# Routing and experts of a soft mixture: fused affine layer norm on VectorE, weight split on GpSimd, second product two steps behind

## The reference, cut to what matters

```python
xn = _layernorm(x, ln_gamma, ln_beta)      # (x - m) * rsqrt(var + eps) * gamma + beta
x_unit = _l2norm(xn, axis=-1)
mu_unit = _l2norm(mu, axis=0)
logits = einsum('bnd,des->bnes', x_unit * scale, mu_unit)
dispatch = softmax(logits, axis=1)                         # over the tokens
combine = softmax(logits.reshape(B, N, E * S), axis=-1)    # over the slots
slot_in = einsum('bnd,bnes->besd', xn, dispatch)
h = gelu(einsum('besd,edh->besh', slot_in, w1) + b1)       # per expert
slot_out = einsum('besh,ehd->besd', h, w2) + b2
out = einsum('besd,bnes->bnd', slot_out, combine)          # x + out is returned
```

## Time and profile before

| | |
|---|---|
| median of 3 runs | 1244.21 us (1241.42 to 1247.08) |
| profiled execution | 1238.86 us, of which the span in the trace is 1236.7 us |
| busy over the span | PE 86%, DVE 74%, ACT 58%, POOL 35% |
| route, about 987 to 1140 us of the span | 16 batches |
| experts, about 1141 to 1194 us | 16 experts |
| combine, about 1194 us to the end | 16 batches |

### The profile page before, as it was taken

The page is one execution under the profiler, slowest core; times in us unless marked ns, Lnnn a source line. Parts: engine busy times, 40 slices in busy tenths (PEclk is TensorE's granted clock), DMA queues, the critical chain, the costliest instruction groups (busy, mean ns, idle before and its releaser), DMA issues. The chain is left out here.

```text
span 1236.7 us, 28303 instructions
## 1 busy us (share of the span) xinstructions
PE 1064.9 (86%) x8053; PEld 1014.9 (82%) x8053; DVE 920.8 (74%) x2388; ACT 715.7 (58%) x2225; POOL 438.3 (35%) x753
## 2 busy tenths in 40 slices
PE   7779999999999997899999548888888747777998
PEld 6679999999999996899999547787887647676777
DVE  4567677777677765777777649989899769997656
ACT  4466666676666664333333237777777526566754
POOL 0223222223222220121212136666566466663015
PEclk9889999999999999899999859888888969889559
DMA  7578940000000000000000235444455000000113
GB/s 236 129 133 243 114 101 0 0 0 0 0 0 0 0 1 6 27 0 0 0 0 0 63 111 153 143 133 140 140 140 146 17 15 2 0 0 1 43 32 122
DMA packets 71574, 73.90 MB, mean 60 GB/s; under 512 B 23025, under 2 KB 63829, under 8 KB 71381
## 3 DMA queue, kind: packets, MB, share of 16 engines
q1 hardware_dynamic: 70692, 72.47, 23.4%
q10 hardware_dynamic: 816, 0.66, 0.2%
HBM read 41.52 MB, written 31.54 MB: 59 GB/s over the span
## 5 line engine op out<-in xcount | busy, mean ns | idle before, releaser
L776 POOL TENSOR_TENSOR att_prob<-att_ex,att_rinv 128x308 f32<-128x308 f32 x128 | 89.9, 702 | 216.1 <-DVE att_rinv L679 202.7
L1051 ACT ACTIVATE att_ex<-att_s_bank,att_mx 128x77 f32<-128x77 f32 x512 | 125.5, 337 | 30.9 <-DVE att_mx L1117 28.9
L1330 ACT ACTIVATE ffn_hid<-ffn_h_bank,ffn_b 128x256 f32<-128x256 f32 x128 | 60.8, 476 | 125.4 <-DVE ffn_hT_lo L1361 65.6
L638 ACT ACTIVATE att_ex<-att_s_bank,att_mx 128x77 f32<-128x77 f32 x512 | 125.0, 333 | 11.4 <-DVE att_mx L669 11.3
L1188 POOL TENSOR_TENSOR att_prob<-att_ex,att_rinv 128x256 f32<-128x256 f32 x128 | 79.1, 618 | 96.4 <-DVE att_rinv L1129 94.6
L702 DVE TENSOR_TENSOR att_pT_lo<-att_t_bank,att_pT_hi 128x512 fp32r<-128x512 f32 x128 | 88.3, 690 | 32.2 <-ACT att_pT_hi L616 31.8
L646 ACT ACTIVATE att_qT<-att_q_bank 128x256 f32<-128x256 f32 x128 | 49.2, 385 | 101.1 <-PE att_q_bank L496 100.0
L516 PE MATMUL att_s_bank<-att_keys,att_qT 128*128 128x154 f32 x512 | 95.0, 309 | 0.0
L616 ACT CAST att_pT_hi<-att_t_bank 128x512 fp32r<-128x512 f32 x128 | 75.0, 587 | 24.2 <-PE att_t_bank L526 19.3
L964 PE MATMUL att_s_bank<-att_ks,att_qs 100*128 100x154 f32 x256 | 54.6, 300 | 39.5 <-ACT att_ex L1051 32.3
L540 PE MATMUL att_o_bank<-att_pT_hi,att_vals_hi 128*128 128x256 f32 x256 | 83.0, 324 | 3.0 <-DVE att_oT_lo L683 2.0
(11 more groups left out here) (274 smaller groups left out, 4174.0 us busy)
## 6 DMA issues: line engine op xcount, KB each, us to landing
att_qs<-q_dram SPq DMA_DIRECT2D x96, 128.0 KB, 2.7
ks_dram<-att_zeros SPq DMA_DIRECT2D x16, 462.0 KB, 5.6
att_ks<-ks_dram SPq DMA_DIRECT2D x16, 462.0 KB, 5.0
all_x<-in_x SPq DMA_DIRECT2D x4, 1024.0 KB, 7.0
att_vd<-vd_dram SPq DMA_DIRECT2D x16, 256.0 KB
q_dram<-att_qT_hi SPq DMA_DIRECT2D x16, 256.0 KB, 2.1
q_dram<-att_qT_lo SPq DMA_DIRECT2D x16, 256.0 KB, 2.1
out<-comb_y SPq DMA_DIRECT2D x16, 256.0 KB, 2.1
```

What stands on the lines that cost most here:

```text
L638: last = nc.scalar.activation(ex[t % RING][:, r, :], s_bank[t % 2][:, r * SK:(r + 1) * SK], ACT.Exp, bias=mx[t % 2][:, r:r + 1])
L776: nc.gpsimd.tensor_tensor(out, e, w, ALU.mult).then_inc(p_ready, 1)
L1051: last = nc.scalar.activation(ex[t % RING][:, r, :], s_bank[t % 2][:, r * SK:(r + 1) * SK], ACT.Exp, bias=mx[t % 2][:, r:r + 1])
```

## The change

In route, the affine layer norm leaves GpSimd. VectorE makes xg = (x - mean) x gamma and xa = xg x rstd + beta by four `scalar_tensor_tensor` instructions of 128x256 (two for each half of the tokens) in place of two `tensor_scalar`. The new `normalise(f+2)` stands after `disp_lo`, and the statistics of f+3 stand behind `transposed_x(f+1)`. GpSimd keeps `split_x`, `inverse_deviation` and `lengths`, in that order.

In experts, GpSimd rounds and subtracts both weights. ScalarE and VectorE keep the slots and the hidden values. `down` runs two steps behind `up` instead of one, with three buffers for `w2` and `hT`. All loops of the phase are written out.

```diff
+            def normalise(f, i):
+                dve.wait_ge(ln.rstd_ready, f + 1)
+                at_least(dve, ln.ready, NC * f)
+                for q in range(NC):
+                    nc.vector.scalar_tensor_tensor(xg[:, q, :], x_rows(st, f, q), ln.mean_var[:, q, 0:1], gamma[:, :],
+                                                   ALU.subtract, ALU.mult).then_inc(xg_ready, 1)
+                at_least(dve, xu_ready, NC * (f - 1))
+                at_least(dve, xas_ready, f - 1)
+                for q in range(NC):
+                    dve.wait_ge(xg_ready, NC * f + q + 1)
+                    nc.vector.scalar_tensor_tensor(xa[i][:, q, :], xg[:, q, :], ln.rstd[:, q:q + 1], beta[:, :],
+                                                   ALU.mult, ALU.add).then_inc(ln.ready, 1)
...
             def batch(f, i, front, back, following, later, latest):
-                if later:
-                    ln.normalise(dve, f + 2, xg_ready, 1)
                 if front:
                     maxima(f, 0)
...
-                if latest:
-                    ln.statistics(dve, f + 3)
+                if later:
+                    normalise(f + 2, i)
                 if front:
                     invert(f, 0)
                 if front:
                     maxima(f, 1)
                 if following:
                     transposed_x(f + 1, 1 - i)
+                if latest:
+                    ln.statistics(dve, f + 3)
                 if front:
                     weigh(f, 0)
                 if front:
...
             def batch(f, i, front, back, following, later, latest):
                 if front:
                     split_x(f, i)
-                if later:
-                    affine(f + 2, i)
                 if latest:
                     ln.inverse_deviation(pool, f + 3)
                 if later:
...
+            for e in range(2, E):
+                sp.wait_ge(w2_lo, e - 1)
+                load_expert(sp, d, st, e, e % 2, w_in[e % 2])
...
+            for e in range(E + LAG):
+                if e < E:
+                    up(e)
+                if e >= LAG:
+                    down(e - LAG)
...
+            round_inputs(0)
...
+            for e in range(E + LAG):
+                if e + 1 < E:
+                    round_inputs(e + 1)
+                if e < E:
+                    hidden(e)
+                if e >= LAG:
+                    outputs(e - LAG)
...
+        @block.gpsimd
+        def _(pool):
+            def split_w1(e):
+                i = e % 2
+                at_least(pool, w_in[i], 32 * (e // 2))
+                at_least(pool, h_psum, e - 1)
+                nc.gpsimd.tensor_copy(w1[i][0][:, :, :], w1_raw[i][:, :, :]).then_inc(w1_hi, 1)
+                pool.wait_ge(w1_hi, e + 1)
+                nc.gpsimd.tensor_tensor(w1[i][1][:, :, :], w1_raw[i][:, :, :], fp32_of(w1[i][0][:, :, :]), ALU.subtract).then_inc(w1_lo, 1)
+
+            def split_w2(e):
+                i, r = e % 2, e % RING
+                at_least(pool, o_psum, e - 2)
+                nc.gpsimd.tensor_copy(w2[r][0][:, :], w2_raw[i][:, :]).then_inc(w2_hi, 1)
+                pool.wait_ge(w2_hi, e + 1)
+                nc.gpsimd.tensor_tensor(w2[r][1][:, :], w2_raw[i][:, :], fp32_of(w2[r][0][:, :]), ALU.subtract).then_inc(w2_lo, 1)
+
+            split_w1(0)
+            for e in range(E):
+                if e + 1 < E:
+                    split_w1(e + 1)
+                split_w2(e)
```

More of the change, by code:

```diff
@@ L1569, in square @@
             def square(f, i):
-                act.wait_ge(xa_ready, f + 1)
+                act.wait_ge(ln.ready, NC * f + NC)
                 for q in range(NC):
@@ L1717, in _ @@
             poolt = Ticking(pool, m.sem("pool_ticks"))
[L1718 to L1728, removed]
             def lengths(f):
@@ L1799, in slots_of, with up @@
         def slots_of(e):
-            return st.slots[:, :, :, bass.ds(e * S, S)]
+            return st.slots[:, :, :, e * S:(e + 1) * S]
         @block.sync
         def _(sp):
[L1804 to L1807, removed]
+            for e in range(2, E):
+                sp.wait_ge(w2_lo, e - 1)
+                load_expert(sp, d, st, e, e % 2, w_in[e % 2])
+            for i in range(2):
+                sp.wait_ge(w_in[i], 32 * (E // 2 - 1))
         @block.tensor
         def _(pe):
-            def up(e, i):
+            def up(e):
+                i = e % 2
+                pe.wait_ge(w1_lo, e + 1)
                 pe.wait_ge(in_lo, e + 1)
@@ L1817, in up, with down @@
                 last.then_inc(h_psum, 1)
-            def down(e, i):
+            def down(e):
+                i, r = e % 2, e % RING
+                pe.wait_ge(w2_lo, e + 1)
                 pe.wait_ge(hid_lo, e + 1)
-                pe.wait_ge(w2_lo, e + 1)
                 at_least(pe, out_stored, DC * (e - 1))
@@ L1824, in down @@
                     for n, (a, b) in enumerate(PASSES):
-                        last = nc.tensor.matmul(o_bank[i][:, c * B * S:(c + 1) * B * S], w2[i][a][:, c * P:(c + 1) * P],
-                                                hT[i][b][:, :], start=n == 0, stop=n == 2)
+                        last = nc.tensor.matmul(o_bank[i][:, c * B * S:(c + 1) * B * S], w2[r][a][:, c * P:(c + 1) * P],
+                                                hT[r][b][:, :], start=n == 0, stop=n == 2)
                 last.then_inc(o_psum, 1)
[L1829 to L1833, removed]
             nc.tensor.transpose(b_bank[0:HID, 0:E], b_raw[:, 0:HID], st.ident[0:E, 0:E])
@@ L1851, in split_w2 @@
[L1851 to L1872, removed]
@@ L1874, in _, with hidden @@
-            split_inputs(0, 0)
-            split_w2(0, 0)
-            act.wait_ge(b_ready, 2)
-            batch_pairs(act, step)
+                nc.scalar.copy(xin[e % 2][0][:, :, :, :], slots_of(e)).then_inc(in_hi, 1)
+            def hidden(e):
+                act.wait_ge(h_psum, e + 1)
+                at_least(act, hid_lo, e - 1)
+                nc.scalar.activation(hid[e % 2][:, :], h_bank[e % 2][0:HID, 0:B * S], ACT.Gelu,
+                                     bias=b1[:, e:e + 1]).then_inc(hid_ready, 1)
@@ new lines, in outputs @@
+            def outputs(e):
+                act.wait_ge(o_psum, e + 1)
+                act.wait_ge(in_lo, e + 1)
+                for c in range(DC):
+                    nc.scalar.activation(st.slots[:, c, :, e * S:(e + 1) * S],
+                                         o_bank[e % 2][:, c * B * S:(c + 1) * B * S].rearrange("p (b s) -> p b s", b=B),
+                                         ACT.Identity, bias=b2[:, c, e:e + 1]).then_inc(out_stored, 1)
+            round_inputs(0)
+            act.wait_ge(b_ready, 2)
```

63 lines of the change are left out of this document (27 added, 36 removed).

## The result

The changed kernel took 1270.18 us (median of 4 runs, 1269.34 to 1271.06), the kernel before 1244.45 us in the same comparison: a ratio of 1.0208 (95% interval 1.0183 to 1.0232), so slower by 2.1% (that it is slower is clear of noise, that it is by more than 2% is not). The forecast was 1276 (1254 to 1294). The profiled execution took 1270.70 us with a span of 1268.7 us, against 1238.86 and 1236.7 before. One execution of before in the later comparisons (1266.54 us, at a granted clock of 0.83 where the others show 0.90 to 0.91) is left out of all figures.

The account below looks back on a forecast made before the run. It took GpSimd's wait for the DMA trip to bound experts and a VectorE-GpSimd chain to bound route. Experts +24.4 and route +8.0 on 1238.86 gave 1271.3; 5.35 for the median gave 1276.6, called 1276 (1254 to 1294).

Parts of the forecast that it names:

- the closed loop: Experts: GpSimd stands still for the DMA trip every turn; turn 4.9 us, the phase +24.4 us.
- Rival C: Blocking between VectorE and GpSimd costs more than booked: turns of 5.4 (experts) and 9.7 (route), 1290 us; chance 0.18.
- the chain over the statistics: Route: VectorE through the statistics, then GpSimd to the next reciprocal, sets a turn of 9.2 us; route +8.0 us.
- the second chain: Route: from reciprocal over top, exponentials and squares to length and the next reciprocal, 8.3 us a turn.
- thirteen turns of 9.2: Route: after the first reciprocal at 1007.3, thirteen turns of 9.2 us and one of 8.3 end at 1135.2.
- The head's gain of 1.9: Start of route: the first top no longer waits for xn(2); gain taken as 1.9 us, between 0 and 3.
- A: Both loops closed as summed: 1276 us, own range 1264 to 1288; chance 0.5.
- D: Route bound by VectorE's work alone, turn 7.3 us, 1252 us in all; chance 0.06.
- Rival B: Route runs at the second chain, turn 8.3 us, 1265 us in all; chance 0.2.
- E: Faster than before: the trip does not close the experts loop, turn stays 3.05 us; 1227 with D's route; chance 0.06.

Follow-up runs that it names:

- Experiment 3: The changed kernel with GpSimd splitting w1(e) then w2(e) in each experts step, no w1 a step ahead: 1245.91 us, 1.0034 of the kernel before.
- Experiment 4: The changed kernel with GpSimd's lengths(f+2) in front of inverse_deviation(f+3) in route: 1260.92 us, 1.0148 of the kernel before.
- experiment 7: Experiment 4 with VectorE's normalise(f+2) moved behind transposed_x: 1259.93 us, 1.0139 of the kernel before.
- experiment 5: The changed kernel with the statistics of f+3 put back behind normalise, ahead of the second top: 1275.85 us, 1.0264 of the kernel before.
- experiment 9: Experiment 8 with both of VectorE's weight pairs ahead of the statistics of f+3: 1231.62 us, 0.99 of the kernel before.
- experiment 6: The changed kernel with one more GpSimd wait, so xaS_lo starts only after the xu pair: 1271.07 us, 1.0231 of the kernel before.
- experiment 8: Experiment 7 with the experts order of experiment 3, w1(e) then w2(e): 1235.20 us, 0.9937 of the kernel before.
- experiment 2: The kernel before with only the new experts phase, route unchanged: 1267.97 us, 1.0213 of the kernel before.

## Why the prediction was right

**Experts, the closed loop: right, and sized right.** The theory was a loop from the split of `w2` over SyncE and the DMA to the next `w1`, with `w2(e-1)` stuck behind that wait. Experiment 3 opened it by order alone, and the whole loss went. Terms, forecast and then measured: trip 2.73 and 2.65; split of `w1` 0.94 with its gaps and 0.77; split of `w2` 1.22 with its gaps and 1.47; turn 4.89 and 4.96. The copy of 256 elements, priced at 0.45 between 0.287 and 0.617, took 0.39 us where it ran alone (experiment 3) and 0.59 beside `xin_lo`; the subtraction of 256, priced at 0.617, took 0.73 and 0.80. The 3.05 us of TensorE in a turn, with which the prediction counts, stands in no row shown there; in the trace of before the first matmuls of `up` are that far apart (33.51 us for the 11 turns from 1155.77 to 1189.28). From the first split to the last matmul I had 76.15 us, and it was 76.25. My addends give 1217.65 for the end and not the 1217.8 that I wrote, so the working says 76.0.

**Rival C's mechanism exists, in small.** GpSimd's split of `w2` was stretched by VectorE's two-input `xin_lo`, by some 0.25 us a turn, and `xin_lo` by it (0.96 for 0.75). Rival C had 0.5. The shorter trip and the quicker split of `w1` made it good in the turn shown (4.79), and all but 0.07 us of it on average.

**Route, the chain over the statistics: right in the loop, mis-sized in the head.** From reciprocal to `var_eps` I had 6.62 us, and it was 6.46 (1062.69 to 1069.15); from there to the next reciprocal 2.64, and it was 2.59. I took 9.2 and the turns of the loop were 9.17. Experiment 4 took the wait for the statistics out of that chain, and the turn fell to 8.2 to 8.8, at its shortest the second chain (8.24, 8.3 in the forecast) with `length` waiting for the squares; there VectorE's own work is nearly as long. The term that was off is "thirteen turns of 9.2": the first three took 23.3 us and not 27.6. In two of them `xu` was not stretched, worth 0.7 us each; in all three GpSimd's small instructions followed each other more closely than in the loop, and that I priced by rows of the loop. The kernel before had shorter turns there too: its first three took 8.05 us on average, the ten behind them 8.68. That is 4.3 of the 5.1 us by which route came out cheaper. Of the rest 0.6 is the last turn (7.70 for 8.3). The head's gain of 1.9 was 1.78.

**Two errors that cancelled.** The profiled execution was forecast at 1271.3 and took 1270.70. That closeness is luck: route was 5.1 us too dear, and 4.5 us ahead of it, which no part of the change touches, were in no sum. So the two terms hid each other, and 1271.3 is not as good as it looks. Then the forecast of the median added 5.35 us for the distance of before's median from its profiled execution; the changed kernel's median lay 0.5 below its own. That is the 6 us between 1276 and 1270. The profiled execution of before was one of its quick ones, and such an offset isn't to be carried over whole.

**The remaining cases.** Two bounds are slips: the turns given for A reach from 1268 to 1285, not from 1264 to 1288, and the range's 1254 lies just above D's 1252, not below. Rival B's turn (8.3) is about what experiment 4 made of the kernel, so B was one line of order away. D would have needed VectorE without gaps. Its 7.3 us of work was a fair floor (7.2 to 7.4 busy in experiment 7), but no kernel here reached it in every turn. E is out: even with experts at 3.04 us a turn (experiment 3) the change stays 0.34% over before. The mechanism that would bring a gain was not in the change but in the two orders.

**Open.** When the granted clock falls: experiments 5, 7 and 9 show it fall in turns with idle TensorE, and not in every such turn. Idle for 2.65 us in experiment 5 and 1.67 in experiment 7 came with 0.50 for the matmuls behind, 1.65 in experiment 7 with 1.00; in experiment 9 a turn with 1.95 us idle had 0.79 and one with 1.97 had 1.00. Experiment 9 removed the long turns together with the gap, which fits, but moved the statistics too; no run varied the gap alone. Why route begins up to 5 us later in some executions wasn't looked into.

## What to carry to other kernels

Before work is moved onto an idle engine, write out that engine's queue beside the queue of the DMAs that feed it: when the item that frees a buffer stands behind an item that needs the refilled buffer, the loop closes, and each turn costs the trip (2.65 us here, 37.1 us of waiting in 14 trips), however idle the engine is. A step that is taken "one ahead" in a queue shared by both needs the other order; one more raw buffer should do as well, which no run here tried. A GpSimd instruction that holds VectorE up is not disarmed by moving it a little: in experiment 6 `xu` won 0.74 us and `xg` lost 0.76. Look at which neighbour it will hit next, and put it beside one that the rows show at its usual length, as `disp_lo` (0.68 us) was beside `xaS_lo`. Price a written-out head by its own turns (7.47 to 8.30 us here), not by those of the loop (9.17).

## What the runs showed of the hardware

- The fused `xg` pair (`scalar_tensor_tensor`, two SBUF inputs) was held up by GpSimd's `xaS_lo` of 1.28 us, as the `xu` pair was: `xg` took 0.87 us free and, beside `xaS_lo`, 1.41 to 1.72 in experiment 4 and 1.57 to 1.89 in experiment 6; `xu` took 0.74 free and 1.48 beside it in the turn shown of the changed kernel. `disp_lo`, which reads one operand from PSUM, was not held up: 0.68 us at 1061.27 in experiment 7, with `xaS_lo` running from 1061.14 to 1062.49, and 0.68 to 0.69 in all of experiments 4, 6 and 7, with `xaS_lo` beside it or not. Whether the operands decide this was not tried by itself.
- The other way round, GpSimd's copy of 64x256 took 0.39 us alone (experiment 3) and 0.59 us beside `xin_lo` (the changed kernel, 1170.96); once, at 1155.44 beside `hT_lo` and a whole `xin_lo` pair, 1.26.
- The granted clock changed with the order of VectorE's work: from 1045 to 1115 us it was 1.00 in the changed kernel and 0.88 in experiment 5, where 2.65 us of idle TensorE came with 12 matmuls at 0.21 us instead of 0.11.
- In experts the granted clock was about one half nearly throughout, whether TensorE idled or not: from 1150 to 1180 us it was 0.50 with 30.0 us busy of 30 in experiments 8 and 9, 0.50 with 18.8 in experiment 2, and 0.53 with 18.0 in the changed kernel, whose first six matmuls of the phase (from 1150.76) were 0.12 us apart and the later ones 0.21. Its matmuls there use 64 rows or 64 columns; whether that is why was not tried.
